# Attention values with the values stationary in 32-column tiles and the probabilities moving

## The chip, the cores and the metric

The kernel runs on one core of a Trainium2 chip. The metric is device time in microseconds (us) of one execution; lower is better.

## The reference

All data are float32. For x of 16 batches of 256 rows by 256, and a context of 77 rows per batch:

```python
x = x + xattn(layernorm(x), ctx)      # 16 heads of 16: softmax(q k^T / 4) v, then @ Wp + bp
# in xattn, per batch and head:
#   scores = einsum('bqhd,bkhd->bhqk', q, k) * scale
#   attn   = softmax(scores); out = einsum('bhqk,bkhd->bqhd', attn, v) @ Wp + bp
x = x + moe(layernorm(x))             # 8 experts, top 2 of a router, gated FFN 256 -> 1024 -> 256
```

The change is in the attention alone: in the product of the softmax numerators with v, the division by their sums, and what hands the result to the projection Wp.

## The kernel before, in words

The 4096 rows of x are 32 tiles of 128 rows. The program is written out by hand, engine by engine, with semaphores. From its start to some 320 us it goes through rounds: one tile per round, software-pipelined, so that in round i TensorE (PE) makes the scores of tile i, the transposed probabilities and the values of tile i-1, the projection of tile i-2, and router work of tiles i-4 and i-5. After the rounds (and over the last of them) come the expert tiles, which keep PE busy to the end and are not touched.

Every engine executes its own list strictly in the order that its round function writes. The parts of a round that matter here:

- **PE**, `round_first` (L1909), `round_second` (L1932), `round_third` (L1949): scores of the first 8 heads (L1755); transposes of xn and xf (L1820, L1876); transposed probabilities, group 0 (L1773); transposed attention output of tile i-2 (`transpose_attn`, L1787); group 1 of the probabilities; then in odd rounds the queries of a batch (L1802), in even rounds its values (L1868), and in every second even round also the keys of two batches (L1858). Then scores of the other 8 heads; group 2 of the probabilities; router logits (L1847); projection (`project`, L1806); `place_pair` in even rounds (L1880); `values` (L1824).
- **ScalarE (ACT)**, `round_ops` (L1114): copies the transposed probabilities from PSUM group by group (`probs_t_copy`, L955, group 2 in two pieces), with `attn_t_copy` (L970) between groups 0 and 1; then `make_y`, the exponentials (`exp_scores`, L950), queries or keys, group 2, `logits_copy`, `make_z`, the second exponential; at the end of the round the copies of xn and xf, `make_xn`, and in even rounds `mark` and `gate_exp`.
- **VectorE (DVE)**, `round_ops` (L1544): maxima and subtraction of the softmax (L1247), statistics, x1, and as one of the last things `normalized` (L1320): the reciprocal of 16 sums per row and the product with the 256 values.
- **GpSimd (POOL)**, `spread_values` (L786): lays v out into block-diagonal tiles with a mask. **SyncE (SP)** loads and stores, `load_values` (L533) among them.

The 1232 keys (16 heads of 77) are cut into 10 blocks of 128, the last with 80. For each block one float32 matmul has the transposed probabilities (128 keys by 128 rows) as its stationary operand, and 2 or 3 heads of v, each with a column of ones behind it, as the moving one (34 or 51 columns). So PSUM gets the values and the sums of a row side by side in `value_bank`. In the trace a float32 matmul is two instructions (passes), each with its own weight load.

```python
for k in range(KB):
    if k % 4 == 0:
        e.wait_ge(probs_t_out, 3 * i + k // 4 + 1)
    mm = e.matmul(value_bank[:, first * VW:(first + nh) * VW], probs_t[i % 2][0:size, k, :],
                  v_blocks[b % 2][0:size, k, 0:nh, :].rearrange("p j d -> p (j d)"), ...)
```

Two PSUM banks, 6 and 7, are handed round between the small users (`misc_turns`, L235); `claim` waits until the user before has been read.

Of the kernel before, what the change touches and what calls it, by code (L numbers as in the profile page):

```python
# [8 lines left out]
F32 = mybir.dt.float32  # L9
# [7 lines left out]
P = 128  # L17
BATCH, SEQ, D = 16, 256, 256
CTX = 77
# [7 lines left out]
NT = TOKENS // P  # L27
# [7 lines left out]
KB = -(-KEYS // P)  # L35
TAIL = KEYS - (KB - 1) * P
BLOCK_HEADS = 3
VW = HD + 1
# [127 lines left out]
C_TOKEN = C_VMASK + KB * BLOCK_HEADS  # L166
# [14 lines left out]
def block_heads(i):  # L181

    first = i * P // CTX
    last = min(i * P + P - 1, KEYS - 1) // CTX
    return first, last - first + 1


def constants():
# [6 lines left out]
    for i in range(KB):  # L195
        first, n = block_heads(i)
        for j in range(BLOCK_HEADS):
            c[:, C_VMASK + i * BLOCK_HEADS + j] = (i * P + p) // CTX == first + j
# [36 lines left out]
def misc_turns():  # L235

    order = []
    for i in range(FIRST_ROUND, LAST_ROUND + 1):
        even, nb = i % 2 == 0, i // 2 + 1
        batch = 0 <= nb < BATCH  # L240
        uses = [("attn", i - 2)] if 0 <= i - 2 < NT else []
# [19 lines left out]
def build(nc, a, out):  # L261
    with ExitStack() as ctx:
# [8 lines left out]
        def sems(name, n):  # L271
# [3 lines left out]
        v_flat = nc.dram_tensor("v_flat", [BATCH, KEYS, VW], F32, kind="Internal").ap()  # L275

        f_const, f_bv, f_rows, f_kv, f_wq, f_wp, f_router = (
            sem(n) for n in ("f_const", "f_bv", "f_rows", "f_kv", "f_wq", "f_wp", "f_router"))
# [7 lines left out]
        (bq_ready, setup_ready, half_ready, zeros_ready, ones_ready, mv_ready, blocks_ready) = (  # L286
            sem(n) for n in ("bq_ready", "setup_ready", "half_ready", "zeros_ready",
                             "ones_ready", "mv_ready", "blocks_ready"))
# [9 lines left out]
        (ctx_t_out, k_out, k_high, xn_t_out, q_out, q_high, exp_made, probs_t_out, attn_t_out,  # L298
         xf_t_out, logits_out) = (
            sem(n) for n in ("ctx_t_out", "k_out", "k_high", "xn_t_out", "q_out", "q_high",  # L300
                             "exp_made", "probs_t_out", "attn_t_out", "xf_t_out", "logits_out"))
        (ctx_t_mm, k_mm, v_mm, xn_t_mm, q_mm, scores_mm, probs_t_mm, values_mm, attn_t_mm, proj_mm,
         xf_t_mm, logits_mm, place_mm) = (
            sem(n) for n in ("ctx_t_mm", "k_mm", "v_mm", "xn_t_mm", "q_mm", "scores_mm",
                             "probs_t_mm", "values_mm", "attn_t_mm", "proj_mm", "xf_t_mm",
                             "logits_mm", "place_mm"))
# [71 lines left out]
        v_sb = [sb(f"v_sb{i}", [CTX, HEADS, VW]) for i in range(2)]  # L378
        v_rep = [sb(f"v_rep{i}", [P, KB, VW]) for i in range(2)]
# [3 lines left out]
        v_blocks = [sb(f"v_blocks{i}", [P, KB, BLOCK_HEADS, VW]) for i in range(2)]  # L383
# [10 lines left out]
        attn = [sb(f"attn{i}", [P, D]) for i in range(2)]  # L394
        attn_t = [sb(f"attn_t{i}", [P, DC, P]) for i in range(2)]
        recip = [sb(f"recip{i}", [P, HEADS]) for i in range(2)]
# [45 lines left out]
        misc_read = {"ctx": lambda b: (ctx_t_out, b + 1), "attn": lambda i: (attn_t_out, i + 1),  # L442
# [56 lines left out]
        def sync_program(e):  # L499
# [33 lines left out]
            def load_values(b):  # L533
                e.wait_ge(f_vstore[b % 2], 16 * (b // 2 + 1))
                if b >= 2:
                    e.wait_ge(v_spread, 6 * (b - 1))
                full = (KB - 1) * P
                e.dma_start(v_rep[b % 2][:, 0:KB - 1, :],
                            v_flat[b][0:full, :].rearrange("(i p) d -> p i d", p=P)).then_inc(
                                f_vload[b % 2], 16)  # L540
                e.dma_start(v_rep[b % 2][0:TAIL, KB - 1, :], v_flat[b][full:KEYS, :]).then_inc(
                    f_vload[b % 2], 16)
# [20 lines left out]
            load_x(4)  # L563
            load_row(f_wp, 1, "bp")
# [168 lines left out]
        def pool_program(e):  # L733
# [52 lines left out]
            def spread_values(b):  # L786
                e.wait_ge(f_vload[b % 2], 32 * (b // 2 + 1))
                if b >= 2:
                    e.wait_ge(values_mm, 2 * b - 2)
                vm = const[:, C_VMASK:C_VMASK + KB * BLOCK_HEADS].rearrange(  # L790
                    "p (i j) -> p i j", i=KB)
                for j in range(BLOCK_HEADS):
                    for parts, lo, hi in ((P, 0, KB - 1), (TAIL, KB - 1, KB)):
                        e.tensor_tensor(
                            v_blocks[b % 2][0:parts, lo:hi, j, :], v_rep[b % 2][0:parts, lo:hi, :],
                            vm[0:parts, lo:hi, j:j + 1].broadcast_to([parts, hi - lo, VW]),
                            ALU.mult).then_inc(v_spread, 1)
# [19 lines left out]
            for i in range(2):  # L817
                e.memset(v_sb[i][:, :, HD:VW], 1.0).then_inc(ones_ready, 1)
# [81 lines left out]
        def act_program(e):  # L900
# [54 lines left out]
            def probs_t_copy(i, g):  # L955
# [5 lines left out]
                if g < 2:  # L961
# [3 lines left out]
                else:  # L965
                    e.activation(probs_t[i % 2][:, k0, :], ps[:, 0:P], ACTF.Copy)
                    e.activation(probs_t[i % 2][0:TAIL, k0 + 1, :], ps[0:TAIL, P:2 * P],
                                 ACTF.Copy).then_inc(probs_t_out, 1)

            def attn_t_copy(i):  # L970
                e.wait_ge(attn_t_mm, i + 1)
                if i >= 2:
                    e.wait_ge(proj_mm, i - 1)
                e.activation(attn_t[i % 2][:, :, :],
                             misc_of("attn", i)[:, 0:DC * P].rearrange("p (c k) -> p c k", c=DC),
                             ACTF.Copy).then_inc(attn_t_out, 1)
# [137 lines left out]
            def round_ops(i):  # L1114
# [1068 lines left out]
```

## Time and profile before

| | us |
|---|---|
| median of 3 runs | 933.84 (932.91 to 934.47) |
| the profiled execution | 936.83 |
| its span in the trace | 935.0 |
| PE busy | 891.6 (95%) |
| DVE busy | 747.5 (80%) |
| ACT busy | 647.7 (69%) |
| POOL busy | 412.6 (44%) |

The profiled execution took 3.0 us more than the median of the runs; its span leaves 1.8 us for what lies around it. Busy time of PE has the modelled tails of matmuls in it, so that the distance between the starts of two groups says better than a duration what a group costs.

### The profile page before, as it was taken

Reading aid. Unit: us, or ns where it says so; the run is one execution under the profiler, and the core shown is the slowest. Engines: PE = TensorE matmul, PEld = TensorE weight load, DVE = VectorE, ACT = ScalarE, POOL = GpSimd, SP = SyncE. Lnnn points to the kernel's source line nnn. Section 1 sums busy time; section 2 is a strip of 40 time slices with the busy share of each in tenths; the row PEclk is TensorE's granted clock in tenths of the full one; section 3 lists DMA queues with packets and bytes.
Section 4 is the critical chain, followed back from the end, with each engine's and each line's share of the span. In section 5 each row is a group of like instructions: output and inputs, shape, how many; then the busy total and the mean of one; then the engine's idle time right before and its main releaser. Section 6 shows DMA issues by size and latency. Waiting matters only on the chain.

```text
span 935.0 us, 19225 instructions
## 1 busy us (share of the span) xinstructions
PE 891.6 (95%) x6206; PEld 800.3 (86%) x6206; DVE 747.5 (80%) x1757; ACT 647.7 (69%) x1305; POOL 412.6 (44%) x649
## 2 busy tenths in 40 slices
PE   4999999999999999999999999999999999999994
PEld 3787888888878887888999999898898998998994
DVE  2677888888888889787979888887877877778883
ACT  3666767677676774776968777766876777677773
POOL 3455577777777667340432230505214234052042
PEclk9899999999999999999999999999999999999998
DMA  5332242343246337643755454826817737465442
GB/s 141 61 69 50 53 106 67 75 108 74 61 116 192 114 106 281 183 116 116 221 142 172 130 166 151 243 91 186 302 25 230 265 77 261 166 179 178 146 80 26
DMA packets 132626, 129.18 MB, mean 138 GB/s; under 512 B 59985, under 2 KB 117409, under 8 KB 132385
## 3 DMA queue, kind: packets, MB, share of 16 engines
q1 hardware_dynamic: 119648, 110.36, 38.2%
q0 software_dynamic: 12864, 17.44, 10.1%
q8 instruction: 55, 0.90, 0.4%
q14 instruction: 59, 0.48, 0.2%
HBM read 102.01 MB, written 25.36 MB: 136 GB/s over the span
## 4 chain that ended last, share of the span: by engine, by line
PE 79%; DVE 7%; ACT 5%; issue 4%; POOL 2%; SPq 1%; DMA 1%; ACTq 0%; DVEq 0%; POOLq 0%
PE bank L2002 35%; PE bank L2046 18%; PE bank L1835 7%; PE bank L1755 3%; PE bank L1994 3%; PE bank L1812 3%; PE bank L1773 2%; PE bank L2034 2%; PE bank L1971 1%; PE bank L1820 1%; DVE maxes L1256 1%; PE bank L1868 1%; PE bank L1858 1%; ACT q_t L943 1%; PE bank L1802 1%
## 5 line engine op out<-in xcount | busy, mean ns | idle before, releaser
L859 POOL DMA_INDIRECT out_rows<-yo,token x68 | 114.3, 1682 | 380.5 <-ACT yo L1111 314.7
L2002 PE MATMUL bank<-xh,wh 128*128 128x512 f32 (+1 forms) x672 | 234.2, 349 | 3.7 <-DVE gate_in L1628 3.1
L2002 PE MATMUL bank<-xl,wh 128*128 128x512 f32 (+1 forms) x672 | 228.4, 340 | 0.0
L2002 PE MATMUL bank<-xh,wl 128*128 128x512 f32 (+1 forms) x672 | 228.0, 339 | 0.0
L1604 DVE TENSOR_TENSOR wl<-raw,wh 128x1024 fp32r<-128x1024 f32 x126 | 152.4, 1220 | 12.9 <-ACT wh L1042 12.0
L2002 PEld LDWEIGHTS bank<-xh,wh 128*128 128x128 f32 x672 | 127.9, 190 | 17.9 <-DVE gate_in L1628 6.0
L2046 PE MATMUL bank<-wh,hh 128*128 128x256 f32 x496 | 142.1, 286 | 0.5 <-DVE yo L1663 0.3
L2046 PE MATMUL bank<-wh,hl 128*128 128x256 f32 x496 | 140.8, 284 | 0.0
L2046 PE MATMUL bank<-wl,hh 128*128 128x256 f32 x496 | 140.8, 284 | 0.0
L2002 PEld LDWEIGHTS bank<-xh,wl 128*128 128x128 f32 x672 | 127.5, 190 | 14.8
L2002 PEld LDWEIGHTS bank<-xl,wh 128*128 128x128 f32 x672 | 128.0, 190 | 10.7
L1042 ACT ACTIVATE wh<-raw 128x1024 fp32r<-128x1024 f32 x126 | 131.1, 1053 | 0.0
L1648 DVE TENSOR_TENSOR hl<-gate_in,hh 128x512 fp32r<-128x512 f32 x128 | 88.0, 687 | 43.7 <-ACT hh L1105 32.7
L1105 ACT ACTIVATE hh<-gate_in 128x512 fp32r<-128x512 f32 x128 | 80.2, 626 | 32.0 <-DVE gate_in L1641 31.6
L1080 ACT ACTIVATE gate_in<-bank,par 128x512 f32<-128x512 f32 x88 | 60.2, 684 | 58.0 <-PE bank L2002 57.9
L2046 PEld LDWEIGHTS bank<-wh,hh 128*128 128x128 f32 x496 | 95.2, 192 | 3.9 <-DVE yo L1663 0.8
L2046 PEld LDWEIGHTS bank<-wl,hh 128*128 128x128 f32 x496 | 95.3, 192 | 2.5
L2046 PEld LDWEIGHTS bank<-wh,hl 128*128 128x128 f32 x496 | 95.3, 192 | 0.0
L1092 ACT ACTIVATE gate_in<-gate_in 128x512 f32<-128x512 f32 (+1 forms) x144 | 86.1, 598 | 0.0
L806 POOL DMA_INDIRECT z_rows<-z,slot x64 | 68.3, 1068 | 22.1 <-issue 17.6
L1256 DVE TENSOR_REDUCE maxes<-bank 128x4 f32<-128x308 f32 x128 | 54.9, 470 | 27.0 <-PE bank L1755 26.4
L1835 PEld LDWEIGHTS bank<-v_blocks,probs_t 128*128 128x128 f32 (+1 forms) x640 | 75.3, 192 | 0.9
(198 smaller groups left out, 1887.4 us busy)
## 6 DMA issues: line engine op xcount, KB each, us to landing
raw<-in_W SPq DMA_DIRECT2D x42, 1024.0 KB, 6.5
raw<-in_Wo SPq DMA_DIRECT2D x25, 1024.0 KB, 5.9
whole<-in_W SPq DMA_DIRECT2D x8, 1024.0 KB, 8.3
xs<-in_x SPq DMA_DIRECT2D x32, 128.0 KB, 2.6
out_rows<-x SPq DMA_DIRECT2D x32, 128.0 KB, 1.8
shared<-z_rows SPq DMA_DIRECT2D x7, 520.0 KB, 5.3
bo_row<-in_bo SPq DMA_DIRECT2D x25, 128.0 KB, 4.4
k_blocks<-k_parts SPq DMA_DIRECT2D x128, 19.2 KB
```

What stands on the lines that cost most here:

```text
L806: e.indirect_dma_start(out=z_rows, out_offset=bass.IndirectOffsetOnAxis(ap=slot[:, 2 * p + t, k:k + 1], axis=0), in_=z[p % ZR][:, t, :], i ...
L859: e.indirect_dma_start(out=out, out_offset=bass.IndirectOffsetOnAxis(ap=token[j % 4][:, s:s + 1], axis=0), in_=yo[j % 2][:, s, :], in_offs ...
L1042: e.activation(wh[split_before(j) % 2][:, w, c, :], raw[w][:, c, :], ACTF.Copy).then_inc(w_high, 1)
L1080: e.activation(dst[:, :], ps[:, 0:WIDTH], ACTF.Identity, bias=par[j % PR][:, X_B2 + u:X_B2 + u + 1]).then_inc(gate_out, 1)
L1092: e.activation(gate_in[n % 3][:, 0:w], gate_in[n % 3][:, 0:w], ACTF.Silu).then_inc(silu_made, 1)
L1105: e.activation(dst, hid[n % 3][:, 0:w], ACTF.Copy).then_inc(hid_high, 1)
L1256: e.tensor_reduce(maxes[i % 2][:, hs], view, AXX, ALU.max).then_inc(max_found, 1)
L1604: e.tensor_tensor(wl[q][:, w, c, :], raw[w][:, c, :], wh[q][:, w, c, :].bitcast(F32), ALU.subtract).then_inc(w_low, 1)
L1648: e.tensor_tensor(hl[n % (HR - 1)][:, :], hid[n % 3][:, :], hh[n % HR][:, :].bitcast(F32), ALU.subtract).then_inc(hid_low, 1)
L1835: mm = e.matmul(value_bank[:, first * VW:(first + nh) * VW], probs_t[i % 2][0:size, k, :], v_blocks[b % 2][0:size, k, 0:nh, :].rearrange(" ...
L2002: mm = e.matmul(ps[:, h * cols:(h + 1) * cols], ws[split_before(j) % 2][:, w, c, m * P:(m + 1) * P], xx[j % 2][:, c, 0:cols], start=(h == ...
L2046: mm = e.matmul(down_bank[s // 2][:, (s % 2) * D:(s % 2 + 1) * D], hs[:, at:at + P], ws[q][:, 2, m // 4, (m % 4) * D:(m % 4 + 1) * D], sta ...
```

## The change

The values become stationary and the probabilities moving. The 616 keys of 8 heads are a half with 5 blocks (128, 128, 128, 128, 104); 10 blocks as before, but none crosses the halves. Two heads are 32 columns; such a tile of v (`v_blocks`, 128 keys by 32) is loaded and 128 columns of transposed probabilities stream against it, into 32 PSUM partitions. The 154 keys of two heads lie in two neighbouring blocks, so 4 pairs of heads, 2 blocks and 2 halves make 16 matmuls. Sums come from 10 more matmuls with a constant selector of 32 columns (`sum_probs`), spread over the four groups of 32 partitions. The output is transposed already, so `transpose_attn` and its copy go. In their place:

1. ACT copies values and sums to SBUF (`sums_copy`, 384 columns) behind the second exponential.
2. PE turns and adds up the partial sums with one float32 matmul at the end of the round (`transpose_sums`).
3. DVE takes the reciprocal of 16 sums (`invert_sums`), where `normalized` stood.
4. ACT widens it to 256 columns (`widen_inverses`), first thing in the next round.
5. PE transposes that (`spread_inverses`) where `transpose_attn` stood.
6. DVE multiplies (`normalize`) behind `xf_sums`, in the first half of the round; the projection waits for it.

On PE `sum_probs` and `values` now stand ahead of `project` and wait for all three groups of the probabilities. Group 2 is copied in one piece. `spread_values` has 4 instructions in place of 6, `load_values` 4 DMAs in place of 2, and SP loads the selector (128 x 336) once.

```diff
 SP
+            e.dma_start(select[:, :], a["select"]).then_inc(f_select, 16)
...
+                for m in range(DC):
+                    first = m * HALF_KEYS
+                    e.dma_start(v_rep[b % 2][:, m, 0:JB - 1, :], ...
+                    e.dma_start(v_rep[b % 2][0:TAIL, m, JB - 1, :], ...
 ACT
+            def sums_copy(i):
+                e.wait_ge(values_mm, i + 1)
+                if i:
+                    e.wait_ge(sums_t_mm, i)
+                    e.wait_ge(attn_made, i)
+                e.activation(sums[:, :], value_bank[:, 0:(DC + 1) * P], ACTF.Copy).then_inc(
+                    sums_out, 1)
+
+            def widen_inverses(i):
+                e.wait_ge(recip_made, i + 1)
+                if i:
+                    e.wait_ge(spread_mm, i)
+                e.activation(inverses[:, :].rearrange("p (h d) -> p h d", h=HEADS),
+                             recip[:, :].unsqueeze(2).broadcast_to([P, HEADS, HD]),
+                             ACTF.Copy).then_inc(inverses_out, 1)
...
+                if 0 <= i - 2 < NT:
+                    widen_inverses(i - 2)
                 if before:
                     probs_t_copy(i - 1, 0)
-                if 0 <= i - 2 < NT:
-                    attn_t_copy(i - 2)
-                if before:
                     probs_t_copy(i - 1, 1)
 DVE
+            def normalize(i):
+                e.wait_ge(sums_out, i + 1)
+                e.wait_ge(spread_mm, i + 1)
                 if i >= 2:
-                    e.wait_ge(attn_t_mm, i - 1)
+                    e.wait_ge(proj_mm, i - 1)
+                e.tensor_tensor(attn_t[i % 2][:, :, :].rearrange("p c k -> p (c k)"),
+                                sums[:, 0:DC * P], misc_of("spread", i)[:, 0:DC * P],
                                 ALU.mult).then_inc(attn_made, 1)
 PE
+            def transpose_sums(i):
+                at = (DC + 1) * P
+                e.wait_ge(sums_out, i + 1)
+                if i:
+                    e.wait_ge(recip_made, i)
+                e.matmul(value_bank[:, at:at + HEADS], sums[:, DC * P:(DC + 1) * P], select[:, S_PICK:S_END],
+                         start=True, stop=True, skip_group_check=True).then_inc(sums_t_mm, 1)
+
+            def spread_inverses(i):
+                ps = claim("spread", i)
+                e.wait_ge(inverses_out, i + 1)
+                for m in range(DC):
+                    mm = e.transpose(ps[:, m * P:(m + 1) * P],
+                                     inverses[:, m * P:(m + 1) * P], ident)
+                mm.then_inc(spread_mm, 1)
...
+            def sum_probs(i):
...
+                e.wait_ge(probs_t_out, 3 * i + 3)
+                for k in range(KB):
+                    q, size = k % QUADS, P if k < KB - DC else TAIL
+                    mm = e.matmul(
+                        value_bank[q * QUAD:(q + 1) * QUAD, DC * P:(DC + 1) * P],
+                        select[0:size, S_SUM + k * QUAD:S_SUM + (k + 1) * QUAD],
+                        probs_t[i % 2][0:size, k, :], start=(k < QUADS),
+                        stop=(k + QUADS >= KB), skip_group_check=True)
+
             def values(i):
...
+                for m in range(DC):
+                    for s in range(2):
+                        for q in range(QUADS):
+                            k, size = block_at(m, q + s), block_rows(q + s)
+                            mm = e.matmul(
+                                value_bank[q * QUAD:(q + 1) * QUAD, m * P:(m + 1) * P],
+                                v_blocks[b % 2][0:size, m, s, q, :, :].rearrange(
+                                    "p h d -> p (h d)"),
+                                probs_t[i % 2][0:size, k, :], start=(s == 0), stop=(s == 1),
+                                skip_group_check=True)
...
                 if 0 <= i - 5 < NT:
                     route_logits(i - 5)
+                if 0 <= i - 1 < NT:
+                    sum_probs(i - 1)
+                    values(i - 1)
                 if 0 <= i - 2 < NT:
                     project(i - 2)
                 if i % 2 == 0 and 0 <= i // 2 - 4 < PAIRS:
                     place_pair(i // 2 - 4)
                 if 0 <= i - 1 < NT:
-                    values(i - 1)
+                    transpose_sums(i - 1)
```

On PE, the second half of an even round, before (the names behind `<-` are what moves and what stands still in the array; L1773 probabilities group 2, L1847 logits, L1812 projection, L1886 to L1891 place, L1835 values, L1755 the next round's scores):

```order
L1773 MATMUL bank<-const,probs 128x128
L1773 MATMUL bank<-const,probs 80x128
L1847 MATMUL bank<-router,xf_t 128x8 x2
L1812 MATMUL bank<-wp,attn_t 128x256 x2
L1886 MATMUL bank<-both,tri 128x16
L1889 MATMUL bank<-off,ones 128x16
L1891 MATMUL bank<-cum,ones 128x24
L1835 MATMUL bank<-v_blocks,probs_t 128x34
L1835 MATMUL bank<-v_blocks,probs_t 128x51
```

The same place in the change (L1825 probabilities, L1920 logits, L1892 sums, L1906 values, L1872 projection, L1959 to L1964 place, L1844 the turned sums, L1805 scores):

```order
L1825 MATMUL bank<-const,probs 104x128 x2
L1920 MATMUL bank<-router,xf_t 128x8 x2
L1892 MATMUL bank<-probs_t,select 32x128 x10
L1906 MATMUL bank<-probs_t,v_blocks 32x128 x16
L1872 MATMUL bank<-wp,attn_t 128x256 x2
L1959 MATMUL bank<-both,tri 128x16
L1962 MATMUL bank<-off,ones 128x16
L1964 MATMUL bank<-cum,ones 128x24
L1844 MATMUL bank<-select,sums 128x16
L1805 MATMUL bank<-k_blocks,q_h 128x308 x2
```

Sums and values moved up to directly behind the logits, 26 matmuls in place of 10; the projection moved behind them, and one small matmul closes the round.

On ACT, from the end of an even round into an odd one, before:

```order
L998 ACTIVATE xn<-xs,shift,scale 128x256
L1022 ACTIVATE z<-const 128x2
L1025 ACTIVATE z<-pick 128x2
L1031 ACTIVATE gates<-gates 128x2
L962 ACTIVATE probs_t<-bank 128x512
L974 ACTIVATE attn_t<-bank 128x256
L962 ACTIVATE probs_t<-bank 128x512
```

and in the change:

```order
L1038 ACTIVATE xn<-xs,shift,scale 128x256
L1062 ACTIVATE z<-const 128x2
L1065 ACTIVATE z<-pick 128x2
L1071 ACTIVATE gates<-gates 128x2
L1014 ACTIVATE inverses<-recip 128x256
L994 ACTIVATE probs_t<-bank 128x512 x2
L1046 ACTIVATE y<-x_2,shift,scale 128x256
L985 ACTIVATE probs<-probs 128x616
L975 ACTIVATE q_t<-bank,bq_scaled 128x256 x2
L980 ACTIVATE q_h<-q_t 128x512
L998 ACTIVATE probs_t<-bank 104x256
```

The copy of the transposed output, which read what PE had made, is gone; an operation that PE waits for stands in front of group 0.

## Rows read from the trace of the kernel before

**Rows 1.** The page: span, and busy time of the engines.
```profile
span 935.0 us, 19225 instructions
PE 891.6 (95%) x6206; PEld 800.3 (86%) x6206; DVE 747.5 (80%) x1757; ACT 647.7 (69%) x1305; POOL 412.6 (44%) x649
```

**Rows 2.** Stretches: us, busy us of PE, PEld, DVE, ACT, POOL (instructions), PE clock, DMA share, GB/s.
```profile
150.00:200.00 50.00, 47.98 (x366) 40.79 (x366) 42.97 (x151) 35.68 (x97) 37.35 (x67) 1.00 0.37 86
```

**Rows 3.** Waits between 80 and 280 us: who waited for whom, us, times, longest.
```profile
PE bank L1812 <- ACT q_t L943: 1.7, 10, 0.2
```

**Rows 4.** PE in time, an odd round: start, us, operation, [idle before].
```profile
183.82 0.41 PE L1755 MATMUL bank<-k_blocks,q_h 64*128 64x308 f32 x2
...
185.37 0.42 PE L1791 MATMUL bank<-const,attn 128*128 128x128 f32 x2
...
186.06 1.89 PE L1802 MATMUL bank<-xn_t,shared 128*128 128x256 f32 x8
187.88 0.41 PE L1755 MATMUL bank<-k_blocks,q_h 64*128 64x308 f32 x2
...
188.78 0.51 PE L1847 MATMUL bank<-router,xf_t 128*128 128x8 f32 x4
189.47 1.13 PE L1812 MATMUL bank<-wp,attn_t 128*128 128x256 f32 x4 [0.18 <-ACT q_t L943]
190.44 2.32 PE L1835 MATMUL bank<-v_blocks,probs_t 128*128 128x34 f32 x20
192.69 0.41 PE L1755 MATMUL bank<-k_blocks,q_h 64*128 64x308 f32 x2
```

**Rows 5.** ACT in time, the same odd round.
```profile
186.27 0.57 ACT L962 ACTIVATE probs_t<-bank 128x512 f32<-128x512 f32 x1
186.74 0.37 ACT L974 ACTIVATE attn_t<-bank 128x256 f32<-128x256 f32 x1
187.01 0.59 ACT L962 ACTIVATE probs_t<-bank 128x512 f32<-128x512 f32 x1
...
187.98 0.72 ACT L953 ACTIVATE probs<-probs 128x616 f32<-128x616 f32 x1
188.58 0.84 ACT L943 ACTIVATE q_t<-bank,bq_scaled 128x256 f32<-128x256 f32 x2
189.46 0.63 ACT L948 ACTIVATE q_h<-q_t 128x512 fp32r<-128x512 f32 x1
```

**Rows 6.** PE in time, the even round behind it, to the next round's start.
```profile
194.25 0.42 PE L1791 MATMUL bank<-const,attn 128*128 128x128 f32 x2
...
196.40 0.41 PE L1755 MATMUL bank<-k_blocks,q_h 64*128 64x308 f32 x2 [0.44 <-DVE probs L1262]
...
197.30 0.51 PE L1847 MATMUL bank<-router,xf_t 128*128 128x8 f32 x4
...
201.02 0.41 PE L1755 MATMUL bank<-k_blocks,q_h 64*128 64x308 f32 x2
```

**Rows 7.** ACT in time, that even round.
```profile
194.83 0.60 ACT L962 ACTIVATE probs_t<-bank 128x512 f32<-128x512 f32 x1
```

**Rows 8.** PE in time, an even round with keys: passes of 154 columns, and pairs of 64-row tiles.
```profile
176.92 1.22 PE L1858 MATMUL bank<-raw,shared 128*128 128x154 f32 x8
177.97 1.02 PE L1868 MATMUL bank<-shared,raw 128*77 128x256 f32 x4
...
181.43 0.17 PE L1889 MATMUL bank<-off,ones 128*128 128x16 bf16 x1
181.46 0.17 PE L1891 MATMUL bank<-cum,ones 128*128 128x24 bf16 x1
...
184.07 0.30 PE L1755 MATMUL bank<-k_blocks,q_l 64*128 64x308 f32 x2
184.21 0.30 PE L1755 MATMUL bank<-k_blocks,q_h 64*128 64x308 f32 x2
184.44 0.33 PE L1820 MATMUL bank<-const,xn 128*128 128x128 f32 x1
```

More of the change, by code:

```diff
@@ L34 @@
 KEYS = HEADS * CTX
[L35 to L38, printed above, removed]
+HALF_KEYS = HPC * CTX
+JB = -(-HALF_KEYS // P)
+KB = DC * JB
+TAIL = HALF_KEYS - (JB - 1) * P
+QUAD = 32
+QH = QUAD // HD
+QUADS = P // QUAD
 WIDTH = 512
@@ L178, with block_at, block_rows, sum_selectors @@
 X_END = X_E + 1
[L181 to L185, printed above, removed]
+S_SUM = 0
+S_PICK = KB * QUAD
+S_END = S_PICK + HEADS
+def block_at(m, j):
+    return m * (JB - 1) + j if j < JB - 1 else DC * (JB - 1) + m
+def block_rows(j):
+    return P if j < JB - 1 else TAIL
+def sum_selectors():
+    c = np.zeros((P, S_END), np.float32)
+    p = np.arange(P)
+    for m in range(DC):
+        for j in range(JB):
+            at = S_SUM + block_at(m, j) * QUAD
+            key = j * P + p[0:block_rows(j)]
+            c[p[0:block_rows(j)], at + m * HPC + key // CTX] = 1.0
+    for q in range(QUADS):
+        c[q * QUAD + np.arange(HEADS), S_PICK + np.arange(HEADS)] = 1.0
+    return c
 def constants():
@@ L194, in constants @@
     c[:, C_IOTA:C_IOTA + P] = p[None, :]
[L195 to L198, printed above, removed]
+    for s in range(2):
+        for q in range(QUADS):
+            for h in range(QH):
+                c[:, C_VMASK + (s * QUADS + q) * QH + h] = (
+                    ((q + s) * P + p) // CTX == q * QH + h)
     c[:, C_TOKEN:C_TOKEN + NT] = p[:, None] + P * np.arange(NT)[None, :]
@@ L382, in build @@
         q_l = [sb(f"q_l{i}", [P, DC, SEQ], F32R) for i in range(2)]
-        v_blocks = [sb(f"v_blocks{i}", [P, KB, BLOCK_HEADS, VW]) for i in range(2)]
+        v_blocks = [sb(f"v_blocks{i}", [P, DC, 2, QUADS, QH, HD]) for i in range(2)]
         probs = [sb(f"probs{i}", [P, HEADS, CTX]) for i in range(2)]
@@ L393, in build @@
         xs = [sb(f"xs{i}", [P, D]) for i in range(XR)]
-        attn = [sb(f"attn{i}", [P, D]) for i in range(2)]
+        select = sb("select", [P, S_END])
+        sums = sb("sums", [P, (DC + 1) * P])
         attn_t = [sb(f"attn_t{i}", [P, DC, P]) for i in range(2)]
-        recip = [sb(f"recip{i}", [P, HEADS]) for i in range(2)]
+        recip = sb("recip", [P, HEADS])
+        inverses = sb("inverses", [P, D])
         x1 = [sb(f"x1_{i}", [P, D]) for i in range(3)]
@@ L1138, in round_ops @@
                     exp_scores(i, 1)
+                if before:
+                    sums_copy(i - 1)
                 if ctx_pair(i) is not None:
@@ L1152, in drain_copies @@
             def drain_copies(i):
+                if i - 2 < NT:
+                    widen_inverses(i - 2)
                 if i - 1 < NT:
                     probs_t_copy(i - 1, 0)
[L1155 to L1157 removed]
                     probs_t_copy(i - 1, 1)
@@ L1539, in dve_program @@
             e.memset(cum[:, 0, :], 0.0)
+            for i in range(2):
+                e.memset(v_rep[i][P - QUAD:P, :, JB - 1, :], 0.0).then_inc(v_rep_ready, 1)
             e.memset(no_sums[:, :], 0.0).then_inc(setup_ready, 1)
@@ L1552, in round_ops @@
                     xf_sums(i - 4)
+                if 0 <= i - 2 < NT:
+                    normalize(i - 2)
                 if i == NT - 1:
@@ L1766, in transpose_probs @@
                 flat = probs[i % 2][:, :, :].rearrange("p h k -> p (h k)")
+                blocks = [(g, j) for j in range(JB - 1)] if g < DC else [
+                    (m, JB - 1) for m in range(DC)]
                 if g == 0:
@@ L1770, in transpose_probs @@
                     e.wait_ge(probs_t_out, v - 1)
-                for j, k in enumerate(range(4 * g, min(4 * g + 4, KB))):
-                    size = P if k < KB - 1 else TAIL
-                    mm = e.transpose(ps[0:size, j * P:(j + 1) * P], flat[:, k * P:k * P + size],
+                for k, (m, j) in enumerate(blocks):
+                    size, first = block_rows(j), m * HALF_KEYS + j * P
+                    mm = e.transpose(ps[0:size, k * P:(k + 1) * P], flat[:, first:first + size],
                                      ident)
@@ L1921, in round_first @@
                 if 0 <= i - 2 < NT:
-                    transpose_attn(i - 2)
+                    spread_inverses(i - 2)
                 if 0 <= i - 1 < NT:
```

135 lines of the change are left out of this document (58 added, 77 removed).

## The prediction

> **What bounds the kernel now.** I read the page first: PE is busy for 95% of the span, DVE for 80%, ACT for 69% [rows 1]. Then the stretches: between 150 and 200 us, amid the rounds that the change touches, PE is busy for 48.0 of 50 us at full clock, DVE for 43.0, ACT for 35.7 [rows 2]. Then the waits: in 200 us of rounds PE's wait of the projection for ACT's queries comes to 1.7 us in 10 waits [rows 3]. So a round costs what PE's list in it costs, and what PE newly waits for is paid in full. Last the order in time. An odd round starts with scores at 183.82 and ends at 192.69: 8.87 us. In it the 20 passes of `values` take 190.44 to 192.69, 2.25 us, 0.1125 us a pass [rows 4]. The even round behind takes 192.69 to 201.02, 8.33 us [rows 4, 6]. ACT looks idle by its share, but in an odd round its list from 186.27 to 190.09 (probabilities, output, exponential, queries; y is left out of the rows) has next to no gap, and the projection already waits 0.18 us for it [rows 4, 5]. There are 31 rounds that hold `values`, which I count all.
>
> **What the change removes and adds on PE.** It removes 20 passes, 2.25 us a round [rows 4]. The two transposes of `transpose_attn` become two of `spread_inverses`: nothing. The turned sums are one float32 matmul with 128 stationary columns, two passes at the 0.1125 us of `values`: +0.23 us. The block size only moves keys between blocks: 10 transposes before and after.
>
> **The 52 narrow passes.** The trace has no 32-column tile, so I bound them. A pass of 256 moving columns takes 0.2275 us (8 queries passes from 186.06 to 187.88 [rows 4]), one of 154 columns 0.131 us (8 passes from 176.92 to 177.97 [rows 8]); that is 0.00095 us a column, and 0.107 us for 128. Above: all one after another, 52 x 0.107 = 5.56 us. Below: tiles side by side. The scores show that tiles can run so: two matmuls in different 64-row halves start together and the next pair comes 0.14 us later [rows 8], no more than 308 columns need. Four abreast are 14 steps (7 matmuls of the fullest group of 32 partitions, two passes each), 1.50 us; and bf16 passes start 0.03 us apart at best [rows 8], which makes 1.56 us of 52. I take a value between: the two passes of one matmul need the same tile, so the second starts 0.107 us behind the first; if matmuls start in program order, the next tile's first pass can only start beside it. Two abreast are 27 steps, 2.89 us. To all but the serial case it adds the passage into the other tiling and back: the first pair of scores takes 0.25 us where the next takes 0.14 (183.82, 184.07, 184.21), and the last 0.23 (to 184.44) [rows 4, 8]; 0.2 us. So X, the time of sums and values, is 3.09 us; the ends are 1.76 and 5.76.
>
> Here the Trainium skill has two rules that speak against one another. The page "TensorEngine Tiling (Array Packing)", section Theoretical Speedup, gives up to 4x for a dimension of at most 32; by it X would be the 1.76 us of the low end. The page "TensorE: Matmul & The Clock Gate", section "Part 3: Packing small matmuls — row/col tiling", says that matmuls start and end strictly in program order; with two passes to a matmul that gives the 3.09 us. The scores' pairs agree with both, since each of them is a single pass; no row here tells the two apart.
>
> **The new wait in the first half.** PE now needs ACT's `widen_inverses` before it can go on to group 1. DVE's reciprocal stands early enough, but in ACT's list the widening stands behind xn and the marks, where group 0 stood: it starts at 186.27 in the odd round [rows 5] and takes what the 256-column `attn_t` took, 0.37 us. So PE passes this point at about 186.7, not 185.37: +1.33 us [rows 4]. In the even round it would start at 194.83 [rows 7] and be ready at 195.25, against 194.25: +1.0 us, of which the 0.44 us that PE waited for DVE in that round cover part [rows 6], so +0.56 us.
>
> **The new wait in the second half.** Before, projection and place stood between the logits and `values` and hid ACT's group 2. Now nothing does. Odd round: PE's queries start 1.33 us later, at 187.4, second scores at 189.2, logits 190.1 to 190.6 (0.90 behind the scores as before, 4 passes about 0.46) [rows 4]. ACT: group 1 at 187.5, the exponential 0.97 behind it (187.01 to 187.98), the queries 0.60 behind that if PE had them; it has them at about 189.35. Then 0.88 to `q_h` (188.58 to 189.46), 0.53 for it (0.63 less what the next overlaps), and group 2 in one piece, like the 0.37 of 256 columns: out at 191.1 [rows 5]. PE starts the sums at 191.2, after a wait of 0.6 us. Then X, the projection 0.97 us (189.47 to 190.44 [rows 4]) and the turned sums 0.23: the round ends at 192.40 + X, where it ended at 192.69. **Odd: X - 0.29.** Even round: second scores at 196.96, logits at 197.86 (0.90 later as before); group 2, transposed just ahead of the logits, is out some 0.15 + 0.37 later at 198.4, sums from 198.45, plus X, 0.97, 0.1 for the three bf16 passes of place [rows 8] and 0.23: 199.75 + X against 201.02 [rows 6]. **Even: X - 1.3.** A round with keys I put between, X - 0.8: PE has more to do there that hides ACT's list, but the bank that v claims is freed by DVE's `normalize` and no longer by a quick ACT copy. The mean of two odd, one even and one with keys is X - 0.67.
>
> What lies beside other work: the copy of values and sums (384 columns, between the 0.37 us of 256 and the 0.59 us of 512 columns [rows 5]) runs under the projection; were that gone, PE would wait it out before the turned sums. DVE keeps the same two operations, reciprocal and product, and has over 10% free. POOL has two mask operations fewer. SP issues two DMAs more in two rounds, ahead of the x1 store and the keys, and the selector once; and a batch's v is laid out two rounds before its first use. If DVE became the bound it would be at 43.0/48.0 of a round, which a longer PE list leaves further off.
>
> **The sum.** X = 3.09 gives +2.42 us a round, x 31 = +75 us, on the profiled execution's 936.8: 1012. The runs' median lies 3.0 lower: **1009 us**. The expert part is unchanged.
>
> **The rivals.**
> - Four abreast (0.25). X = 1.76, +1.09 us a round, +34 us: **968 us**. For it: the scores' pairs show tiles abreast; against it: there each matmul is one pass. It is slower all the same, since the two waits cost more than X saves.
> - One after another (0.14). X = 5.76 less 0.67, +5.09 a round, +158 us: **1092 us**. For it: nothing in the trace has tiles abreast that share the 128 rows, and each of the four streams reads all 128 partitions. This is also the case where the change doesn't do what it says.
> - Faster (0.05). Four abreast without the passage (1.56 us) and both waits hidden, because ACT runs ahead of where I put it: 1.56 + 0.23 - 2.25 = -0.46 us a round, -14 us: **920 us**. With the waits as reckoned it would need X below 0.67 us, 13 ns a pass, under the 30 ns between bf16 starts [rows 8]. So it decides on the waits: they must fall from 1.35 us a round (what is left of X - 0.67 beside X, 0.23 and 2.25) to below 0.46. Against it: ACT's list from 186.27 on has no gap.
> - No change (0.02): waits halved and X near 1.76 by chance.
>
> **Chances and range.** Two abreast has 0.54, between 967 us (waits gone, 3.09 + 0.23 - 2.25 = 1.07 a round) and 1039 us (the 0.131 us of 154 columns for each of 27 steps, X 3.7, and waits a quarter larger: 3.4 a round). Four abreast reaches from 947 us (waits half as long) to 982 (X 2.2). The range of 950 to 1040 us holds both but for the last few us and leaves out serial, faster and no change. A measurement of this kernel tells 0.2% from no change: faster 0.05, same 0.02, slower 0.93.
>
> **What the profile would show.** Right: `sum_probs` and `values` together take about 3.1 us from the first start to the projection; PE idles 1.0 to 1.3 us a round before `spread_inverses` for ACT's `inverses`, and 0.2 to 0.6 us before `sum_probs` for `probs_t`; a mean round of 11.2 us. Wrong: 52 passes in under 2 us (968), or above 5 (1092); no wait before `spread_inverses` would take 1 us a round off; a wait of the projection for DVE, or of the turned sums for ACT's copy, would be one that I left out.

## The result and the profile after

The changed kernel takes 981.87 us (median of 4 runs, 978.8 to 984.83) where the kernel before, on the same chip, takes 934.15 (4 runs, 932.91 to 935.64). The ratio is 1.051, 95% interval 1.0474 to 1.0546: **slower by 48 us**. The forecast was slower by 75, its range 950 to 1040. The profiled execution took 981.41 us.

The page of the kernel after, beside [rows 1]:

```profile
span 979.6 us, 21500 instructions
PE 888.5 (91%) x7294; PEld 782.9 (80%) x7294; DVE 738.0 (75%) x1759; ACT 669.0 (68%) x1305; POOL 408.3 (42%) x615
```

PE is busy for 3 us less although it has 1088 instructions more; the span is 44.6 us longer, so all of the loss is idle time. The stretches show it too (columns as in [rows 2]); the second row takes all the rounds:

```profile
150.00:200.00 50.00, 41.52 (x496) 33.56 (x496) 34.21 (x127) 34.38 (x84) 32.13 (x54) 1.00 0.34 82
32.00:352.00 320.00, 264.58 (x3179) 214.88 (x3180) 220.67 (x777) 211.89 (x498) 180.45 (x317) 1.00 0.31 74
```

PE had 48.0 busy us in 50 [rows 2] and has 41.5, at full clock. What it waits for between 30 and 355 us (who waited for whom, us, times, longest), and what DVE waits for in the same time:

```profile
PE bank L1851 <- ACT inverses L1014: 34.3, 31, 2.4
PE bank L1892 <- ACT probs_t L998: 13.9, 26, 1.0
PE bank L1941 <- DVE attn_t L1376: 3.6, 5, 1.2
...
DVE x L1335 <- PE bank L1872: 56.6, 30, 4.8
```

The first two are the two waits of the forecast. The last one is not in it. In the kernel before, DVE waited for the projection 2.5 us in 3 waits:

```profile
DVE x L1292 <- PE bank L1812: 2.5, 3, 1.1
```

An odd round on PE, to be laid beside [rows 4] (L1851 spread, L1892 sums, L1906 values, L1872 projection, L1844 turned sums):

```profile
186.31 0.41 PE L1805 MATMUL bank<-k_blocks,q_h 64*128 64x308 f32 x2
...
189.28 0.41 PE L1851 MATMUL bank<-const,inverses 128*128 128x128 f32 x2 [1.25 <-ACT inverses L1014]
...
192.67 0.51 PE L1920 MATMUL bank<-router,xf_t 128*128 128x8 f32 x4
193.80 0.74 PE L1892 MATMUL bank<-probs_t,select 128*32 128x128 f32 x18 [0.63 <-ACT probs_t L998]
194.28 0.30 PE L1906 MATMUL bank<-probs_t,v_blocks 128*32 128x128 f32 x2
194.35 0.30 PE L1892 MATMUL bank<-probs_t,select 104*32 104x128 f32 x2
194.41 1.12 PE L1906 MATMUL bank<-probs_t,v_blocks 128*32 128x128 f32 x30
195.46 1.13 PE L1872 MATMUL bank<-wp,attn_t 128*128 128x256 f32 x4
196.43 0.29 PE L1844 MATMUL bank<-select,sums 128*128 128x16 f32 x2
196.57 0.47 PE L1835 MATMUL bank<-const,raw 77*128 77x77 f32 x4
196.96 0.41 PE L1805 MATMUL bank<-k_blocks,q_h 64*128 64x308 f32 x2
```

The 52 narrow passes take 193.80 to 195.46, **X = 1.66 us**, 32 ns each. Without the 0.39 us of the context's transposes (196.57 to 196.96) the round is 10.26 us. The odd round before it has no such transposes and takes 10.33:

```profile
166.43 0.41 PE L1805 MATMUL bank<-k_blocks,q_h 64*128 64x308 f32 x2
...
176.76 0.41 PE L1805 MATMUL bank<-k_blocks,q_h 64*128 64x308 f32 x2
```

The odd round of [rows 4], also without them, is 8.87, and the forecast's rule, X - 0.29, gives 8.87 + 1.37 = 10.24.

What follows from the projection's new place, on DVE:

```profile
196.63 0.42 DVE L1335 TENSOR_TENSOR x<-bank,xs 128x256 f32<-128x256 f32 x1 [1.83 <-PE bank L1872]
...
197.98 0.24 DVE L1368 RECIPROCAL recip<-bank 128x16 f32<-128x16 f32 x1
...
200.40 0.86 DVE L1299 TENSOR_REDUCE maxes<-bank 128x4 f32<-128x308 f32 x2
...
202.28 0.40 DVE L1376 TENSOR_TENSOR attn_t<-sums,bank 128x256 f32<-128x256 f32 x1
```

and on PE, in that round, which has keys (it ends at 208.38):

```profile
202.74 1.09 PE L1941 MATMUL bank<-shared,raw 128*77 128x256 f32 x4 [1.19 <-DVE attn_t L1376]
...
208.38 0.41 PE L1805 MATMUL bank<-k_blocks,q_h 64*128 64x308 f32 x2
```

DVE stands idle for 1.83 us until the projection hands it x. Routing and the reciprocal then fall into the next round, its softmax begins 3.44 us after the round's start (196.96), and v's claim waits 1.19 us for the product. The round takes 11.42 us.

### The profile page after: what moved, and what is told of

Same layout as the page of the kernel before. It is cut to its first block, busy times and chain, and to the rows that moved or that the text cites. A ratio compares the mean times of both kernels' runs of the same rounds, so it can differ in the third digit from the quotient of the medians.

```text
span 979.6 us, 21500 instructions
## 1 busy us (share of the span) xinstructions
PE 888.5 (91%) x7294; PEld 782.9 (80%) x7294; DVE 738.0 (75%) x1759; ACT 669.0 (68%) x1305; POOL 408.3 (42%) x615
## 3 DMA queue, kind: packets, MB, share of 16 engines
q8 instruction: 64, 1.05, 0.5%
## 4 chain that ended last, share of the span: by engine, by line
PE 73%; DVE 9%; ACT 6%; issue 6%; POOL 2%; SPq 2%; DMA 1%; ACTq 0%; DVEq 0%; POOLq 0%
PE bank L2078 33%; PE bank L2122 17%; PE bank L2070 3%; PE bank L1872 3%; PE bank L1906 3%; PE bank L1892 2%; PE bank L1862 2%; PE bank L1805 2%; PE bank L2110 1%; PE bank L2047 1%; DVE maxes L1299 1%; PE bank L1825 1%; PE bank L1941 1%; SPq L553 1%; ACT probs_t L998 1%
## 5 line engine op out<-in xcount | busy, mean ns | idle before, releaser
L840 POOL DMA_INDIRECT z_rows<-z,slot x64 | 70.7, 1104 | 21.8 <-issue 17.7
L1678 DVE SCALAR_TENSOR_TENSOR gate_in<-bank,par,gate_in 128x512 f32<-128x512 f32 x88 | 65.6, 745 | 8.5 <-ACT gate_in L1132 8.5
```

The costliest lines, as they stand in the source:

```text
L840: e.indirect_dma_start(out=z_rows, out_offset=bass.IndirectOffsetOnAxis(ap=slot[:, 2 * p + t, k:k + 1], axis=0), in_=z[p % ZR][:, t, :], i ...
L1678: e.scalar_tensor_tensor(h[:, :], ps[:, 0:WIDTH], par[j % PR][:, X_B1 + u:X_B1 + u + 1], g[:, :], ALU.add, ALU.mult).then_inc(hid_made, 1)
```

## The experiments

The kernel before took 934 to 943 us from chip to chip, so every number below is a ratio to it on the same chip. Runs of one letter were made together on one chip, each letter on another. The changed kernel, run again beside the runs f (f1), has 1.048; it was not run on the chip of the runs e, so that a difference of e1, e2 or e3 to it is one between two chips. The letters in an expectation are those of its own theories; what counts is the number beside each.

**e1: the widening early.** ACT makes the wide inverses at the end of the round before, ahead of xn's copy.

```
-                if 0 <= i - 2 < NT:
-                    widen_inverses(i - 2)
...
+                if before:
+                    widen_inverses(i - 1)
```

> The changed kernel with one edit on ACT: widen_inverses of tile i-1 stands at the end of round i, ahead of the copy of xn, in place of standing behind make_xn at the start of round i+1. Theory A (the loss is PE's waits on the new hand-overs): PE's wait before spread_inverses, 34.3 us over 31 rounds, goes; some comes back as a longer wait before the sums, since ACT's list is no shorter: 982 falls by 20 to 34 us, to 948 to 962 us, and spread_inverses starts without a wait in nearly all rounds. Theory B (ACT's and DVE's lists set the length of a round, and PE's waits only show it): the wait moves to another place and the time stays at 975 to 985 us.

Measured 1.0564 (1.0514 to 1.0615): no gain. On ACT, then on PE:

```profile
216.07 0.42 ACT L1014 ACTIVATE inverses<-recip 128x256 f32<-128x256 f32 x1 [2.73 <-DVE recip L1368]
216.39 0.37 ACT L963 ACTIVATE xn_t<-bank 128x256 f32<-128x256 f32 x1
```
```profile
216.81 0.44 PE L1851 MATMUL bank<-const,inverses 128*128 128x128 f32 x2 [1.04 <-ACT xn_t L963]
...
224.41 0.87 PE L1906 MATMUL bank<-probs_t,v_blocks 128*32 128x128 f32 x19 [1.13 <-issue]
```

ACT waited 2.73 us for DVE's reciprocal and held xn's copy back behind it. The widening is late because the reciprocal is, not only because of ACT's list: DVE's x, ahead of the reciprocal, had waited 1.99 us for the projection. A gap of 1.13 us inside the burst is new; there is nothing in the profile that PE waited for. Such gaps come to 16 us between 30 and 355 us, and to 0.6 us in the changed kernel. They are nearly as large as the gain that theory A wanted (20 to 34 us), so that e1 by itself doesn't say what the early widening is worth; f4 has it without most of them.

**e2: only the order undone.** Projection and place stand ahead of sums and values again; the turned sums stand right behind values.

```
-                if 0 <= i - 1 < NT:
-                    sum_probs(i - 1)
-                    values(i - 1)
...
+                if 0 <= i - 1 < NT:
+                    sum_probs(i - 1)
+                    values(i - 1)
```

> The changed kernel with PE's old order: projection and place ahead of sums and values, the turned sums right behind the values. Theory A: the wait before the sums (13.9 us in all) goes, but the turned sums now wait for ACT's copy with nothing in between, about 0.65 us in each of 31 rounds, +20 us: 980 to 995 us. Theory C (it is the late projection that costs, since DVE's x1 waits for it and pushes its list, the reciprocal with it, into the next round): 960 to 972 us, and DVE's wait of x1 for the projection (37 us between 80 and 280 us) shrinks to a few us.

Measured 1.0547 (1.05 to 1.0594). PE's waits between 30 and 370 us:

```profile
PE bank L1851 <- ACT inverses L1014: 30.1, 27, 2.5
PE bank L1844 <- ACT sums L1007: 19.8, 32, 0.6
```

The turned sums now wait 0.6 us for the copy of the sums in every round: right behind values nothing covers it. The changed order had that cover in the projection. The spread waits nearly as before (34.3 in the changed kernel). DVE's wait for the projection is down to 2.8 us, as theory C wanted, and the time is theory A's all the same. So undoing the order alone moves the loss, it doesn't remove it.

**e3: neighbours in the same tile.** All matmuls of one 32-column tile stand together, so passes that start in program order could not overlap.

```
-                for k in range(KB):
+                for k in sorted(range(KB), key=lambda k: k % QUADS):
...
-                    for s in range(2):
-                        for q in range(QUADS):
+                    for q in range(QUADS):
+                        for s in range(2):
```

> The changed kernel with the 26 matmuls in another order: all matmuls into one group of 32 PSUM partitions stand behind one another, then the next group. If matmuls start in program order across tiles, tiles overlap only at the borders, and the 52 passes take about 52 x 0.107 = 5.5 us in place of 1.66, +3.9 us in 31 rounds, about +120 us: 1100 us. If tiles run each from its own queue, with passes picked out of program order as far as the window reaches, sums and values stay near 1.7 us and the time at 975 to 990 us. In between, a window shorter than the 14 passes of a group: 2 to 4 us.

Measured 1.0639 (1.0591 to 1.0687). A burst on PE:

```profile
169.47 0.89 PE L1892 MATMUL bank<-probs_t,select 128*32 128x128 f32 x14 [0.22 <-ACT probs_t L998]
170.12 0.27 PE L1906 MATMUL bank<-probs_t,v_blocks 128*32 128x128 f32 x1
170.15 0.32 PE L1892 MATMUL bank<-probs_t,select 104*32 104x128 f32 x3
...
170.35 1.13 PE L1906 MATMUL bank<-probs_t,v_blocks 128*32 128x128 f32 x30
171.40 1.13 PE L1872 MATMUL bank<-wp,attn_t 128*128 128x256 f32 x4
```

This burst takes 1.93 us, where one pass after another would be 52 x 0.107 = 5.6 [rows 4, 8]. A pass of values (170.12) starts before three that the program has ahead of it (170.15). So passes for a free tile start ahead of passes that stand before them in the program. Of the 32 bursts 21 take 1.93 us. Ten, every second one from 135 to 337 us, take 2.9 to 3.7 us, with gaps as in e1 (13.7 us in all between 30 and 355 us). So of the some 15 us by which e3 lies above f1's ratio, the 0.27 us in these 21 bursts explain 6, and the gaps can explain the rest. Whether the new order brings the gaps about is not shown.

**e4: the order alone, on the kernel before.** values(i - 1) goes ahead of the projection and place; nothing else of the change is in.

```
+                if 0 <= i - 1 < NT:
+                    values(i - 1)
...
-                if 0 <= i - 1 < NT:
-                    values(i - 1)
```

> The kernel before with one part of the change alone: values stands ahead of projection and place. Theory A: values now waits for ACT's group 2, though only from its ninth matmul on, and the projection comes 2.25 us later for DVE's x1; 0.2 to 0.5 us a round: 940 to 950 us. If the order costs nothing (the loss is all in the new hand-overs): 933 to 936 us.

Measured 1.0373 (1.0326 to 1.0419): 38 us for a change of order. DVE's and PE's waits between 30 and 350 us, the stretch of the rounds, and one round on PE:

```profile
DVE x L1292 <- PE bank L1812: 71.0, 29, 6.3
...
PE bank L1791 <- DVE attn L1328: 14.6, 20, 1.2
```
```profile
32.00:352.00 320.00, 294.01 (x2077) 247.63 (x2076) 222.40 (x779) 198.58 (x500) 183.22 (x348) 0.91 0.32 74
```
```profile
104.19 2.05 PE L1812 MATMUL bank<-wp,attn_t 128*128 128x256 f32 x4
```

DVE waits for the projection as in the changed kernel, and PE then for DVE's product. The granted clock is 0.91 in the mean (0.99 before), and the projection's four passes take 2.05 us where they take 1.13 [rows 4]. That is the lower of the two levels, 1.2 GHz, so PE's 294 busy us of 320 hide passes at half speed. What the clock took can be estimated from these two means: at most 0.08 x 320 = 26 of the 38 us. The waits would be the rest, some 12 us, which is the size that the expectation gave them; it had left out the clock. In the changed kernel the clock stayed at 1.00: there it is idle time alone.

**f1: the changed kernel again.**

> The changed kernel unaltered, as the yardstick beside the three that follow and for the four before, whose chip gave 942 us for the kernel before: a ratio of 1.047 to 1.055 to the kernel before by either theory, and on a chip that gives 942 us some 990 us.

Measured 1.0479 (1.0461 to 1.0496).

**f2: the projection first, and the turn late.** e2, and the turned sums move behind the next round's first scores. The reciprocal follows behind the softmax's first input, the widening behind the copy of the first probabilities, the spread behind keys, values and queries, and the product ahead of the softmax's second input.

```
+                if 0 <= i - 2 < NT:
+                    transpose_sums(i - 2)
...
-                if 0 <= i - 1 < NT:
-                    transpose_sums(i - 1)
```

> The changed kernel with its hand-overs placed anew: projection and place ahead of sums and values as before; the turned sums in the next round behind the first scores; the reciprocal on DVE behind the first softmax half; the widening on ACT behind group 0; spread_inverses behind keys, values or queries; normalize ahead of the second softmax half. Theory A (PE's list is 0.36 us a round shorter: 52 passes in 1.66 us and 0.23 for the turned sums, against 2.25; all the loss is waits): a ratio of 0.985 to 1.00 to the kernel before, with under 0.3 us a round of wait before spread_inverses and the sums. Theory B (the lists of ACT and DVE set the round): the waits stand elsewhere and the ratio stays above 1.03.

Measured 1.0223 (1.02 to 1.0246), 23 us under f1 and between the two theories. A part of what is left sits in rounds with keys:

```profile
185.37 0.44 PE L1853 MATMUL bank<-const,inverses 128*128 128x128 f32 x2 [2.40 <-ACT raw L952]
...
190.73 2.12 PE L1909 MATMUL bank<-probs_t,v_blocks 128*32 128x128 f32 x30
```

The spread waited 2.40 us for the copy of the keys, which stands in ACT's list behind y, and behind that wait the burst runs at half speed: 2.12 us for the 30 passes that take 1.12 elsewhere. In 13 odd rounds the logits waited for the copy of the queries, 7.6 us in all.

**f3: the wait inside the burst.** The first 8 sums and 14 of the values need only the first two copies of the probabilities; the last two sums and two values alone wait for the third.

```
-                e.wait_ge(probs_t_out, 3 * i + 3)
+                e.wait_ge(probs_t_out, 3 * i + 2)
...
+                    if (m, s, q) == late[0]:
+                        e.wait_ge(probs_t_out, 3 * i + 3)
+                        sum_probs(i, range(KB - DC, KB))
```

> The changed kernel with the 26 matmuls parted: those on groups 0 and 1 of the probabilities (8 of the sums, 14 of the values) wait only for these, and the last 4 wait for group 2. Theory A: the wait before the sums (13.9 us in 31 rounds) goes, since 44 passes take 1.4 us and the wait is at most 1.0: 12 to 14 us under the changed kernel, ratio about 1.037. Theory B: within 4 us of the changed kernel.

Measured 1.0372 (1.035 to 1.039): 10 us under f1. The wait of the sums, 14.0 us in f1, is gone; that of the spread stays at 36.0:

```profile
PE bank L1851 <- ACT inverses L1014: 36.0, 32, 2.4
```

**f4: f3, the widening early, and the reciprocal ahead of routing's sums on DVE.**

```
+                if 0 <= i - 1 < NT:
+                    invert_sums(i - 1)
...
-                if 0 <= i - 1 < NT:
-                    invert_sums(i - 1)
```

> The changed kernel with the early widening of e1_widen_early, DVE's reciprocal moved up to right behind x1, and the parted sums of f3_wait_inside. Theory A with a late reciprocal (in e1 ACT waited 2.7 us for it, since DVE's x1 comes late): the widening ends before xn is to be copied, both waits go: 30 to 45 us under the changed kernel, ratio 1.00 to 1.02. Theory C (the late projection costs, through x1, whatever is done to the reciprocal): it stays above 1.03.

Measured 1.0313 (1.0264 to 1.0363): 3 us under f3 by the medians, which is not clear of its own scatter (961 to 972 us). The spread's wait fell from 36.0 to 1.7 us, but others took its place, v's claim first:

```profile
PE bank L1944 <- DVE attn_t L1376: 9.4, 5, 2.6
PE bank L1805 <- DVE probs L1305: 6.9, 6, 1.5
```

With most of both waits of the forecast taken away (1.7 and 5.4 us are left of 34.3 and 14.2), 32 of 45 us remain. The granted clock is 0.97 between 32 and 352 us, where f3 has 0.99, and that can be at most 6 us of them. DVE still waited 58 us for the projection. So the two waits are for the most part places where PE feels that other engines are late.

**g1: f2 without its waits.** ACT copies the keys ahead of y, the logits take the spread's bank in odd rounds, and the reciprocal goes ahead of the softmax's input.

```
+                if batch and even and nb % 2 == 0:
+                    keys(nb // 2)
                 if 0 <= i - 3 < NT:
                     make_y(i - 3)
-                if batch and even and nb % 2 == 0:
-                    keys(nb // 2)
```

> f2_turn_behind_scores with three small moves: ACT copies the keys ahead of y (in f2 y waited for POOL, and spread_inverses for the keys' copy behind it, 2.4 us in a keys round, with PE's clock at half for the round after); in odd rounds the logits take the bank of spread_inverses, not that of the queries (0.6 us of wait in each); DVE's reciprocal ahead of the first softmax half. Theory A: of f2's 22 us over the kernel before, 13 rounds x 0.6 and 7 rounds x 2.4 us and the slow stretches behind them go: ratio 0.99 to 1.00. Theory B: 1.015 to 1.025, as the waits move on.

Measured 1.0079 (1.005 to 1.0108), between the two theories. Starts of an even round, an odd one (then context's transposes, 0.42 us) and one with keys, and the next:

```profile
156.49 0.41 PE L1808 MATMUL bank<-k_blocks,q_h 64*128 64x308 f32 x2
...
164.76 0.41 PE L1808 MATMUL bank<-k_blocks,q_h 64*128 64x308 f32 x2
...
173.86 0.41 PE L1808 MATMUL bank<-k_blocks,q_h 64*128 64x308 f32 x2
...
183.25 0.41 PE L1808 MATMUL bank<-k_blocks,q_h 64*128 64x308 f32 x2
```

8.27 and 9.39 us for the even round and the one with keys, against 8.33 [rows 4, 6] and 9.15; the odd one has 9.10 with the transposes and 8.68 without, and an odd round of the kernel before 9.16 with them and 8.87 without [rows 4]. With little wait in it, the new list of PE costs about what the old one did. X and the turned sums should be 0.36 us under the 2.25 of the old values; where most of that goes was not tested.

**g2: the same edit of ACT's list on the kernel before.**

> The kernel before with one of the three moves alone, ACT's keys ahead of y, as the control for g1. No PE wait of the kernel before stands on it (the claim behind the keys' bank is the logits', 1.2 us later): 0 to 2 us either way by both theories.

Measured 0.9967 (0.9947 to 0.9986), 934.86 us (10 runs) against 937.89 (13): the one kernel here that beats the kernel before, by 0.3%, a little more than the 0 to 2 us expected. PE's waits in its trace are not shorter, so where the 3 us come from stays open.

**h1 and h2: g1 with the projection behind values, and g1 again beside it.**

```
+                if 0 <= i - 1 < NT:
+                    sum_probs(i - 1)
+                    values(i - 1)
...
-                if 0 <= i - 1 < NT:
-                    sum_probs(i - 1)
-                    values(i - 1)
```

> g1_turn_no_claim_waits with one thing put back as the changed kernel has it: sums and values ahead of projection and place. Sums now wait for ACT's group 2 (0.63 us in an odd round of the changed kernel), and DVE's x1 comes 1.66 us later. If the late projection costs what the changed kernel's even rounds and rounds with keys exceeded the forecast by (0.86 and 1.4 us in one round of four each, 0.57 us a round, 18 us in all), and the open wait 0.45 us a round, 14 us: 20 to 32 us over g1, ratio to the kernel before 1.03 to 1.04. If it costs only the open wait: 10 to 15 us. If neither matters: g1's time.

> g1_turn_no_claim_waits unaltered, as the yardstick for h1 on the same chip: ratio to the kernel before 1.005 to 1.011 by every theory.

h1 has 1.058 (1.0531 to 1.0631), h2 1.01 (1.0068 to 1.0132): the order alone costs 48 us here, where 20 to 32 were expected. DVE's wait for the projection, in h1 and in h2, between 30 and 350 us; and in h1 a burst with gaps and the stretch of the rounds:

```profile
DVE x L1338 <- PE bank L1875: 87.2, 29, 6.2
```
```profile
DVE x L1338 <- PE bank L1875: 7.1, 4, 3.7
```
```profile
173.22 0.68 PE L1910 MATMUL bank<-probs_t,v_blocks 128*32 128x128 f32 x4 [0.91 <-issue]
174.69 1.09 PE L1910 MATMUL bank<-probs_t,v_blocks 128*32 128x128 f32 x12 [0.79 <-issue]
175.71 2.08 PE L1875 MATMUL bank<-wp,attn_t 128*128 128x256 f32 x4
```
```profile
32.00:352.00 320.00, 277.89 (x3027) 219.00 (x3026) 213.72 (x757) 203.17 (x489) 175.64 (x311) 0.94 0.30 73
```

The clock is 0.94 here and 0.99 in h2, which can be 0.05 x 320 = 16 us. The waits without a releaser come to 20 us in h1 and 9 in h2, 11 more. So by this estimate some 21 of the 48 us are left for the waits on other engines. In g1, the same kernel as h2 on another chip, such waits come to 0.2 us: they are not a property of the program alone.

## Why the forecast was right in its sign and 27 us too high

**X was mis-sized.** The step "the second starts 0.107 us behind the first; if matmuls start in program order, the next tile's first pass can only start beside it" gave 3.09 us. Measured: 1.66, 0.032 us a pass, four tiles abreast. The row at 194.28, a pass of values, starts ahead of the one at 194.35, a pass of the sums, and e3 shows it over a longer stretch of program. The low end, four tiles abreast, was the right model: 14 steps of 0.107 and the passage of 0.2 are 1.70 (its 1.76 came from the 30 ns between bf16 starts). By the forecast's own signs, under 2 us for the 52 passes meant this rival (968); it was right in X and wrong in the total. The size: 1.43 us x 31 = 44 us too much. (The high end of 5.76 holds the passage of 0.2 us, which the text gives to all but the serial case; nothing hangs on it.)

**The two new waits were right.** Forecast 1.33 us and 0.6 in the odd round, measured 1.25 and 0.63, and the rule X - 0.29 holds to 0.02 us in the one round and 0.09 in the other.

**A term was missing: the projection's lateness.** The even round is 176.76 to 186.31 = 9.55 us, where 8.33 + X - 1.3 gives 8.69; the one with keys 11.42, where 9.15 + X - 0.8 gives 10.01. In the even round:

```profile
179.46 0.41 PE L1851 MATMUL bank<-const,inverses 128*128 128x128 f32 x2 [0.97 <-ACT inverses L1014]
...
181.53 0.41 PE L1805 MATMUL bank<-k_blocks,q_h 64*128 64x308 f32 x2 [0.36 <-DVE probs L1305]
```

PE waits for the inverses as long as forecast (1.0 us), but the wait for DVE's softmax, of which the forecast let 0.44 us cover part of it, is still there, since DVE is later too. The step that failed is "DVE keeps the same two operations, reciprocal and product, and has over 10% free". Free time was no cover: DVE works through a list in order, x stands in it, and x comes 1.66 us of burst later. Reciprocal, softmax and product follow, and PE waits for their results in the next round. For the round with keys the forecast named v's claim on the product and gave it no price beside "PE has more to do there that hides ACT's list"; it measures 1.19 us.

**The sum again.** The first and the last of the 32 bursts start at 32.66 and 308.83 us before (values) and at 32.26 and 350.55 after (sums): 31 rounds of 8.91 and of 10.27 us, +1.36. The forecast with X = 1.66 has 1.66 - 0.67 = +0.99. So 0.37 us a round are left, 11 us in all, which I put down to lateness; it is more in the rounds above, those with v and keys, and no run measures it by itself. Then 2.5 of the 44.6 us of the span lie outside these rounds, and 3.5 in the step from the profiled execution to the median. 1009 - 44 + 11 + 2.5 + 3.5 = 982. That the forecast came within 27 us is in part luck: 44 too much and 17 too little.

**What the order costs.** e4 (+38 us on the old values) and h1 (+48 on the new ones) show that placing values ahead of the projection is enough for a loss of this size in either kernel. Much of it comes there with the lower clock and, in h1, with gaps that have no releaser; the changed kernel has neither, so that these runs don't measure the order's share of its 48 us. That undoing the order alone (e2) brought nothing fits the other half of the change: the sums, turned right behind values, put their copy by ACT on PE's path (19.8 us). Only both together (f2, 23 us), without the waits in ACT's list (g1), bring the time back to 1.008. PE's matmuls are the same in the changed kernel, f2 and g1, so its loss lay in where the list has them and the hand-overs around them.

## What to carry to other kernels

Before one moves a step back in an in-order list, follow its result through every engine to the next round: an engine with free time still passes the delay on. Taking away the wait that stands out (f4) moved most of it to the next consumer, while placing producer and hand-overs anew (f2, g1) gave the time back. Waits can also bring a lower granted clock with them, which by the estimate from e4 cost more than the waits. And where two neighbours of a list each hide the other's latency, undoing either one alone can look worthless.

## What the runs showed of the hardware

- Float32 matmuls in four 32-column tiles run abreast although each is two passes: 52 passes of 128 columns in 1.66 us. Starts go out of program order between tiles. This speaks against the Trainium skill, page "TensorE: Matmul & The Clock Gate", section "Part 3: Packing small matmuls — row/col tiling", by which matmuls start and end strictly in program order; the measurement decides. It bears out the up to 4x of its page "TensorEngine Tiling (Array Packing)", section Theoretical Speedup.
- The order within a burst matters little: 1.93 us with all neighbours in one tile, in the 21 bursts of e3 that have no gap and run at full clock.
- The granted clock fell where PE had stood idle: passes of double length behind a wait of 2.40 us (f2) and behind repeated gaps of 0.8 to 0.9 us (h1, mean 0.94 over the rounds). In the changed kernel, with waits of 1.25 and 0.63 us a round, it stayed at 1.00.
- Gaps of 0.8 to 1.3 us inside bursts, for which the profile shows no releaser: 16 us in e1, 14 in e3, 20 in h1, all waits of that kind counted, but 0.6 in the changed kernel. The same kernel has 0.2 us of them in g1 and 9 in h2. A burst has 104 instructions in 1.66 us. Whether their supply fails there was not tested; the cause is open.
